# A loop over the middle blocks written out on every engine, and no-operations taken from TensorE's stream of small tiles

## What is computed

```
x = layernorm(x + attn(x, Wq, Wk, Wv, Wg, Wp))            # causal within 64 tokens, gated
x = layernorm(x + xattn(x, ctx_512, Wq, w_kc_q, w_kc_kv, W_qr, W_kr, Wo))
x = layernorm(x + ffn(x, gate_weight, gate_up_proj, down_proj))   # 32 experts, top 8

# attn:  s = (q @ k^T) * mask ; o = s @ v, gated, @ Wp
# xattn: q_big = rope(x @ Wq @ w_kc_q) ; q_r = q_big @ W_qr ; k_r = rope(ctx) @ W_kr
#        softmax(q_r @ k_r^T) @ rope(ctx) @ w_kc_kv, @ Wo      (16 heads)
# ffn:   h = silu(x @ g) * (x @ u) ; out += h @ d * routing weight, over experts
```

## Time and profile before

| | |
|---|---|
| time, median of 3 runs | 906.95 us (905.99 to 907.01) |
| the profiled execution | 906.57 us |
| its span, first to last instruction | 904.8 us |
| TensorE busy | 849.5 us, 94% of the span |
| VectorE busy | 636.6 us, 70% |
| ScalarE busy | 280.6 us, 31% |
| GpSimd busy | 126.5 us, 14% |
| mean granted clock of TensorE | 0.984 |

### The profile page before, as it was taken

One profiled execution on the slowest core, in us unless ns is written; L12 is line 12 of the kernel. 1 busy time (PEld: TensorE's weight loads), 2 busy tenths in 40 slices (PEclk: granted clock), 3 DMA queues, 4 the chain that ended last, 5 costly groups with the idle time before them and its releaser, 6 DMA issues.

```text
span 904.8 us, 15074 instructions
## 1 busy us (share of the span) xinstructions
PE 849.5 (94%) x5696; PEld 669.2 (74%) x5696; DVE 636.6 (70%) x1390; ACT 280.6 (31%) x502; POOL 126.5 (14%) x101
## 2 busy tenths in 40 slices
PE   5989999998999989999797999999999999999994
PEld 4967678675786767777565788888888888888873
DVE  3565787876878788779677876656666666656557
ACT  5521143211431124220353423223332323232232
POOL 2023401333013330133113100000000000000021
PEclk9999999999999999999898999999999999999997
DMA  9210000100001000000310041010302021000001
GB/s 353 97 36 1 1 3 1 47 2 17 3 1 47 1 17 1 1 25 4 125 61 23 1 130 61 23 65 1 111 18 70 0 81 40 23 1 1 1 24 70
DMA packets 12692, 35.90 MB, mean 40 GB/s; under 512 B 1488, under 2 KB 2384, under 8 KB 12112
## 3 DMA queue, kind: packets, MB, share of 16 engines
q1 hardware_dynamic: 12624, 34.98, 11.0%
HBM read 30.33 MB, written 2.36 MB: 36 GB/s over the span
## 4 chain that ended last, share of the span: by engine, by line
PE 81%; DVE 12%; issue 3%; ACT 1%; POOL 1%; DMA 0%; ACTq 0%; DVEq 0%; POOLq 0%; another core or an unknown queue 0%
PE ps L243 20%; PE ps L244 19%; PE ps L245 19%; PE ps L1404 6%; PE ps L1486 4%; PE ps L1477 2%; PE ps L1284 2%; PE ps L1462 1%; PE ps L1453 1%; PE ps L1320 1%; PE ps L1238 1%; POOL roped L727 1%; DVE prod L1028 1%; DVE small L255 1%; DVE stats L927 1%
## 5 line engine op out<-in xcount | busy, mean ns | idle before, releaser
L500 DVE TENSOR_TENSOR su<-sg,ps 128x512 f32<-128x512 f32 x96 | 66.0, 688 | 133.3 <-PE ps L245 132.1
L243 PE MATMUL ps<-y_hi,f_hi 128*128 128x512 f32 x384 | 150.9, 393 | 0.0
L244 PE MATMUL ps<-y_lo,f_hi 128*128 128x512 f32 x384 | 150.0, 391 | 0.0
L245 PE MATMUL ps<-y_hi,f_lo 128*128 128x512 f32 x384 | 150.0, 391 | 0.0
L370 ACT ACTIVATE sg<-ps 128x512 f32<-128x512 f32 x96 | 57.4, 598 | 264.6 <-PE ps L245 264.6
L727 POOL TENSOR_TENSOR roped<-prod 128x512 f32<-128x512 f32 x64 | 80.8, 1285 | 175.8 <-DVE prod L1028 175.8
L1028 DVE TENSOR_TENSOR prod<-ps,ropeq 128x512 f32<-128x512 f32 x128 | 79.4, 683 | 26.8 <-PE ps L245 26.3
L245 PEld LDWEIGHTS ps<-y_hi,f_lo 128*128 128x128 f32 x384 | 72.5, 189 | 15.3
L244 PEld LDWEIGHTS ps<-y_lo,f_hi 128*128 128x128 f32 x384 | 72.5, 189 | 15.0
L243 PEld LDWEIGHTS ps<-y_hi,f_hi 128*128 128x128 f32 x384 | 72.5, 189 | 15.0
L243 PE MATMUL ps<-xT_hi,a_hi 128*128 128x512 f32 x192 | 78.4, 408 | 2.8 <-DVE xT_lo L953 2.8
(11 more groups left out here) (157 smaller groups left out, 1372.2 us busy)
## 6 DMA issues: line engine op xcount, KB each, us to landing
cb<-routing SPq DMA_DIRECT2D x32, 256.0 KB
f_raw<-in_L_ffn_gate_up_proj SPq DMA_DIRECT2D x8, 768.0 KB, 5.3
f_raw<-in_L_ffn_down_proj SPq DMA_DIRECT2D x8, 384.0 KB, 5.9
xb<-in_x SPq DMA_DIRECT2D x4, 512.0 KB, 3.8
lq<-in_L_xattn_Wq SPq DMA_DIRECT2D x1, 2048.0 KB, 13.9
x2T_all<-in_L_xattn_Wo SPq DMA_DIRECT2D x1, 2048.0 KB, 8.0
x2T_all<-x2T SPq DMA_DIRECT2D x4, 512.0 KB, 3.3
out<-res SPq DMA_DIRECT2D x4, 512.0 KB, 2.6
```

The lines of the kernel that those rows point to most:

```text
L243: pe.matmul(dst, l_hi, r_hi, start=first, stop=False, skip_group_check=check)
L244: pe.matmul(dst, l_hi, r_lo, start=False, stop=False, skip_group_check=check)
L245: return pe.matmul(dst, l_lo, r_hi, start=False, stop=last, skip_group_check=check)
L500: dve.tensor_tensor(su[:, k % 2], sg[:, k % 2], bank(2 * (k % 2) + 1), ALU.mult).then_inc(s_su, 1)
```

## The change

The loop over the middle blocks is written out in the program, so that b is a plain number everywhere: three copies of `cross(b)` and `pairs(b + 1)` stand one behind the other on each engine, and SyncE's loop over the loads is written out too. No register operation and no branch is left in this part. The no-operations ahead of the tiles are taken away, and the waits move to what follows.

```
-    def over_blocks(eng, linear, pairs, cross):
+    def over_blocks(linear, pairs, cross):
         linear(0)
         pairs(0, False, True)
-        with eng.Fori(0, LAST - 1) as b:
+        for b in range(LAST):
             cross(b, True)
-            pairs(b + 1, True, True)
-        cross(LAST - 1, True)
-        pairs(LAST, True, False)
+            pairs(b + 1, True, b + 1 < LAST)
         cross(LAST, False)
...
         next_x(0)
-        with sp.Fori(0, LAST - 1) as b:
+        for b in range(LAST):
             next_kv(b)
             keep_x2(b)
-            next_x(b + 1)
+            if b + 1 < LAST:
+                next_x(b + 1)
             keep_c(b)
-        next_kv(LAST - 1)
-        keep_x2(LAST - 1)
-        keep_c(LAST - 1)
...
                         pe.wait_ge(s_rp, 24 * b + 3 * p + 3)
-                    if k < 3:
-                        pe.nop(nofuse=True)
                     for h in range(2):
...
                     pe.wait_ge(s_sub, 8 * b + 2 * t)
-                pe.nop(nofuse=True)
                 for p in range(PAIRS):
                     if t == 0:
                         pe.wait_ge(s_lq, 8 * b + p + 1)
-                        pe.nop(nofuse=True)
```

More of the change, by code:

```diff
@@ L739, in cross @@
                         f_lo_out(pool, 0, 0)
-        over_blocks(pool, linear, pairs, cross)
+        over_blocks(linear, pairs, cross)
         ffn_pool(pool)
@@ L913, in cross @@
                 y_hi_out(act, 2)
-        over_blocks(act, linear, pairs, cross)
+        over_blocks(linear, pairs, cross)
         ffn_scalar(act, x2T_out)
@@ L1226, in cross @@
                 norm2(b, 3)
-        over_blocks(dve, linear, pairs, cross)
+        over_blocks(linear, pairs, cross)
         ffn_vector(dve, own, shift_logits, route)
@@ L1564, in cross @@
                 project(3)
-        over_blocks(pe, linear, pairs, cross)
+        over_blocks(linear, pairs, cross)
         ffn_tensor(pe, turn_x2, logits)
```

## The result

The changed kernel takes 900.53 us, median of 6 runs (897.86 to 901.46), against 907.01 (905.99 to 907.44, 6 runs) before: a ratio of 0.993, 95% interval 0.9918 to 0.9943. The profiled execution took 901.3 us, its span is 899.5, its mean granted clock 0.986.

A forecast was written before the change was run, and what follows sets the result against it. The prediction took TensorE, with 81% of the chain of waits, as the bound. Its terms, 2.98 + 0.59 + 0.33 + 0.18 + 0.36 = 4.44 us, gave 902.5 us against the median, range 900.8 to 905.0.

The forecast's parts named there:

- The branch back: TensorE's idle gap at line 620's loop branch, before the next cross's transposes, goes when written out: 2.98 us.
- 74 ns for VectorE's branch: VectorE's loop branch was read as 74 ns at the most, lying under TensorE's branch.
- The second and first time round: First transposes of cross to latent_q(6): 0.59 us for slow clock and register operations second time, 0.33 for register operations first.
- The no-operations: Ahead of tiles in latent_q and scores; one on the path per block, in latent_q(7): 4 x 0.09 = 0.36 us.
- The rival of the tiles: Mid-stream waits on tile matmuls in latent_q and scores(0) hold up the tiles: 907.2 or 916 us; chance 0.08.
- The supply's rival: TensorE not supplied in time with the longer straight code: 911 us, or 905.4 for one gap; chance 0.05.
- What the prediction said that the profile after would show: Transposes about 1.4 us after latent_q(7)'s last records, clock 1.00 into cross(1), scores(0) 1.16 us, copies 104.1 us.
- The end of `pairs` in the loop: TensorE waits for GpSimd, whose register wait costs 0.09 us in each of two iterations: 0.18 us.
- The rival that the clock falls another way: The half-clock stretch in cross(3) gets longer or shorter, 1.7 us at the most: 900.8 or 904.2 us; chance 0.13.

The follow-up runs named there:

- the second experiment: Changed kernel with VectorE alone put back in the hardware loop with register waits for b = 0 and 1; 902.92 us, ratio 0.9944 to the kernel before.
- the first experiment: Kernel before with the middle blocks written out on every engine but the no-operations ahead of the tiles kept; 899.72 us, ratio 0.9927.
- the moved `rms`: Changed kernel with VectorE's rms of the next block moved from pair 6 to pair 3 of pairs(b); 900.72 us, and 901.24 us when run again.

## Why the prediction was right in direction and too small

**The branch back** was right to the hundredth, 2.98 us, and TensorE's own, as its loop alone shows (4.26 us against 1.46, with a branch of 3595 ns). The other engines' branches are hidden, as the second experiment shows for VectorE. But the prediction's 74 ns for VectorE's branch is a misreading: the record is that short, and yet the first operation of the loop's body comes only 2.8 us after it. With VectorE alone in the loop (branch at 213.0, first operation of the second time round at 215.9; in the trace before 212.3 and 215.1):

```profile
L621 DVEq FUSED_REGOPS  x2: 74/74/74, 104.2 to 215.9; - x2
L621 DVEq COMPARE_BRANCH  x2: 55/64/74, 213.0 to 322.4; - x2
```

It costs nothing here, for VectorE has products queued until 215.2 in the trace before, and then waits for TensorE.

**The second and first time round** were right: 0.61 for 0.59 and 0.36 for 0.33. The start of `cross(1)` runs at 1.00. `scores(0)` takes 1.16 us wherever it was slower before, here in block 0:

```profile
110.16 1.16 PE L1445 MATMUL ps<-bdT,lq 64*64 64x64 f32 x64
```

**The no-operations** were right: 0.10 us each by the first experiment, where 0.09 was taken, and at most 0.06 us in a whole copy for all those in mid-stream.

**The rival of the tiles** fell. The 1024 records of line 1398 have a median of 376 ns, the smallest duration that line 1404 had the earlier trace rows, with 64 waits in mid-stream now on them, and the copies need 104.09 to 104.11 us where straight code with no-operations needed 104.12:

```profile
L1398 PE MATMUL ps<-roped,m_w x1024: 376/376/427, 66.8 to 434.9; 64*64 64x256 f32 x171
```

**The supply's rival** fell too: straight code shows no new gap, in any of the three copies.

What the prediction said that the profile after would show came out in every point.

**The step that failed is "The end of `pairs` in the loop".** It said that TensorE waits there for GpSimd, costed GpSimd's register wait at 0.09 and stopped, 0.18 us for two iterations. The releaser was named rightly, and what it adds is 0.08 us by its own start behind VectorE's product, 0.14 by the difference of two kernels. But GpSimd itself waits for VectorE's product, and VectorE works without a break up to it, so the register waits in VectorE's dependent chain move the end of `pairs` as well. Two of them cost 0.44 us together by its timeline, and all of VectorE's 0.43 and 0.45 by the two experiments that take them away and put them back. The term was mis-sized, 1.17 us measured for 0.18, the no-operations apart. With it the sum is 5.4 to 5.5 us and the forecast would have been 901.5 us. The range's lower end, which stood one slow stretch (1.7 us) below the forecast, would have moved to 899.8, and the measured 900.53 lies above that.

The remaining 1.0 us, 901.5 to 900.53, lies within what differs between runs of one kernel. From profiled execution to profiled execution there is no remainder: 5.27 us, where the table has 5.53. The rival that the clock falls another way was right as to the place, `cross(3)`: its first stretch at 0.50 was 6.8 us before, 3.4 in the one trace after and 10.2 in the other. The before kernel's runs in the later sets have mean clocks of 0.980 to 0.987, the changed kernel's 0.985 to 0.991. Part of that is the stretch behind the branch, which is gone for good and is counted in the 0.61. The rest I put down to fewer stretches at the 1.2 GHz level in block 0 and `cross(3)`, on the average of runs. That is argued and not shown: only one execution in each run is traced, no experiment held the clock fixed at no cost, and the kernel before takes different times at one mean clock, which the clock alone doesn't explain.

What stays open is why TensorE's branch back costs 3.6 to 3.8 us. The trace holds a second loop, that of the experts, whose body is about half as many instructions; its longest branch in the changed kernel is this:

```profile
L276 PEldq COMPARE_BRANCH  x2: 83/162/241, 680.8 to 778.8; - x2
```

So it isn't the branch as such but something that goes with this loop's body. VectorE agrees: 2.8 us from its branch back to the body's first operation in this loop, 0.3 in the experts' loop, whose body is shorter for it too (189 records against 321, for TensorE without its matmuls 468 against 1038). But GpSimd and ScalarE go back in this same loop in under 0.3 us, over 51 and 86 records. The Trainium skill's page "Runtime: NRT & Kernel Launch", section "Instruction fetch mechanics", would have it that a target outside the held window must be fetched; TensorE's two loops fit that, but no run here varied the length of a body.

## What to carry to other kernels

When a trace says that the bound engine waits for engine X, go on and ask what X waited for, until an engine that has no idle time before the place; every cost on that one's dependent chain counts, however short its operations. Where a kernel holds the same work in a loop and in straight code, the difference of copies gives a price to some hundredths of a microsecond (the straight copies of these traces lie between 104.07 and 104.16 us); where the straight copy does other work, as at the end of `pairs(3)`, compare the operations one by one, and start and end with the same record, or the control misleads as it did for the moved `rms`. Work that only keeps the clock up must fit in the idle time; count the records that it makes before choosing how much.

## What the runs showed of the hardware that I had not expected

- A wait on a register in VectorE's chain of short dependent operations costs 0.10 us in one place and 0.34 in another (0.31 and 0.55 us from start to start against 0.21). Ahead of GpSimd's held-up sum it costs 0.08 (0.16 us behind VectorE's product against 0.08), and ahead of TensorE's `latent_q(7)` 0.09, which here lies in another wait.
- The held-up tile starts 0.05 us behind its releaser with the wait on itself (ScalarE's 214.84 + 0.60 = 215.44, start 215.49; GpSimd's 216.11, start 216.16), and 0.14 or 0.15 behind GpSimd or ScalarE through a no-operation. Behind ScalarE in the loop, with the target in a register, it is 0.24.
- Two traces of one kernel on the same code agree to 0.02 us in undisturbed stretches of 104 us, and differ by 2.1 and 1.8 us in the two stretches where the granted clock fell at one time and not, or for longer, at the other. The 2.1 us, over one slow stretch of 3.4 us, are more than the 1.7 that half the clock can cost there. The changed kernel's twelve times follow its mean clock closely; the forty of the kernel before do not.
- The Trainium skill's "Advanced Engine Details and Errata", section "Control Flow Timing", gives 108 ns for a compare-and-branch. On TensorE, VectorE, ScalarE and GpSimd the branches that fell through, and those back in the experts' loop, took 40 to 252 ns by their records, below it or about twice it; TensorE's back over the long body took 3595 to 3771. A short record doesn't prove a cheap branch: VectorE's took 74 ns, and its sequencer's next operation came 2.8 us after it.
